# An attention and mixture-of-experts block: choosing the four experts by replacing them, finding slots by sorting, and keeping every routing weight behind its token's row

## What is computed

```python
scores = sigmoid(X @ gate_w.T)                       # 8192 x 32
_, idx = top_k(scores + bias, K)                     # four experts of a token
w = take_along_axis(scores, idx)                     # their scores, without the bias
w = w / clip(sum(w, -1), 1e-12)
eid = idx.reshape(-1)
pos = cumsum(onehot(eid)) - 1 at eid                 # how many came to this expert before
valid = pos < C                                      # later ones are dropped
xe[eid, pos] = X of the token, where valid
h  = silu(xe @ W1) * (xe @ W3);  ye = h @ W2         # each expert on its 512 slots
out = sum over the four choices of ye[eid, pos] * w  (0 where not valid)
out = out + silu(X @ sw1.T) * (X @ sw3.T) @ sw2.T    # shared expert
```

## Time and profile before

| | |
|---|---|
| median of three runs | 2133.41 us (2128.07, 2134.71, 2133.41) |
| the profiled execution | 2129.57 us |
| its span, first to last instruction | 2127.8 us |
| mean granted TensorE clock | 0.947 |
| busy share of the span: PE, DVE, ACT, POOL | 86%, 57%, 53%, 36% |
| first and last scatter of the routing (L1260) | start at 995.94 and 1451.96 us |
| first gather of the experts (L1412) | starts at 1456.45 us |

### The profile page before, as it was taken

How to read it: one execution, slowest core, us unless ns; L and a number is a source line. 1 busy time by engine, 2 the same in 40 slices (tenths; PEclk the granted TensorE clock), 3 DMA queues, 4 the chain that set the end, 5 groups by cost and what they waited for, 6 DMA issues and landing times.

```text
span 2127.8 us, 33721 instructions
## 1 busy us (share of the span) xinstructions
PE 1833.3 (86%) x12976; PEld 890.8 (42%) x12976; DVE 1207.1 (57%) x2230; ACT 1125.4 (53%) x1371; POOL 759.8 (36%) x718
## 2 busy tenths in 40 slices
PE   8899999999988999699788988545999989897785
PEld 6444444444436888123233333222444444443332
DVE  6676666666650000158788888861444434345886
ACT  5555554545525666568677777422444444442343
POOL 0000000000000000013787788875677777761110
PEclk9999999999998999899999999857999999999997
DMA  7435353455328887567787775443799999877983
GB/s 253 153 109 205 105 172 142 135 179 174 127 88 218 211 212 201 125 171 210 206 243 237 217 218 189 160 184 101 180 201 213 245 241 240 198 155 230 339 291 140
DMA packets 188848, 405.15 MB, mean 190 GB/s; under 512 B 33812, under 2 KB 72084, under 8 KB 172064
## 3 DMA queue, kind: packets, MB, share of 16 engines
q1 hardware_dynamic: 83184, 222.41, 35.4%
q10 hardware_dynamic: 68640, 124.26, 16.8%
q0 software_dynamic: 36864, 56.32, 13.9%
HBM read 237.06 MB, written 177.08 MB: 195 GB/s over the span
## 4 chain that ended last, share of the span: by engine, by line
PE 13%; DVE 12%; DMA 11%; issue 11%; POOL 8%; ACT 4%; SPq 1%; POOLq 0%; DVEq 0%; ACTq 0%
POOL slot_dram L1260 4%; PE s_gates L1485 3%; DMA acc_dram<-s_y,s_slot 3%; PE s_ups L1485 3%; DMA s_spread<-share_dram 2%; PE s_ys L1500 2%; DMA s_rows<-rows_dram,s_slot 2%; POOL acc_dram L1426 2%; DMA den_dram<-s_den 2%; ACT s_xT L1531 1%; DVE s_stats L1651 1%; DVE s_x L1670 1%; PE s_y L898 1%; PE s_turned L1462 1%; POOL s_rows L1412 1%
## 5 line engine op out<-in xcount | busy, mean ns | idle before, releaser
L258 PE MATMUL s_proj<-s_xT,keep_wqkv 128*128 128x512 f16 x1536 | 341.8, 379 | 0.0
L1260 POOL DMA_INDIRECT slot_dram<-keep_filled,keep_slots x256 | 293.4, 1146 | 98.2 <-issue 70.3
L1426 POOL DMA_INDIRECT acc_dram<-s_y,s_slot x128 | 202.9, 1585 | 96.2 <-DVE s_y L1627 42.1
L258 PEld LDWEIGHTS s_proj<-s_xT,keep_wqkv 128*128 128x128 f16 x1536 | 147.8, 98 | 183.2 <-issue 12.6
L898 PE MATMUL s_y<-keep_wo,s_at_hl 128*128 128x512 f16 x768 | 189.1, 399 | 37.7 <-ACT s_z L988 37.7
L237 PE MATMUL s_proj<-keep_wqkv,s_xT 128*128 128x512 f16 x768 | 180.5, 394 | 34.5 <-ACT s_xT L500 34.5
L1540 ACT ACTIVATE s_gate<-s_gates 128x512 f32<-128x512 f32 x96 | 57.1, 597 | 261.9 <-PE s_ups L1485 216.5
L339 POOL TENSOR_SCALAR s_rstd<-s_mv 128x4 f32<-128x4 f32 x16 | 16.0, 999 | 496.7 <-DVE s_mv L354 496.7
L1610 DVE SCALAR_TENSOR_TENSOR s_h<-s_gate,s_ups 128x512 f32<-128x512 f32 x96 | 65.8, 686 | 213.6 <-ACT s_gate L1540 213.6
L518 ACT ACTIVATE s_hl<-s_rot 128x1024 f16<-128x1024 f32 x64 | 67.6, 1057 | 221.8 <-DVE s_rot L400 221.3
L387 DVE TENSOR_TENSOR s_by_cos<-s_proj,s_table 128x1024 f32<-128x1024 f32 x64 | 78.3, 1224 | 172.2 <-PE s_proj L258 172.2
(11 more groups left out here) (165 smaller groups left out, 3209.8 us busy)
## 6 DMA issues: line engine op xcount, KB each, us to landing
s_x<-x_in SPq DMA_DIRECT2D x32, 1024.0 KB, 13.1
qk_dram<-s_hl ACTq DMA_DIRECT2D x32, 1024.0 KB, 5.9
keep_ahead<-qk_dram SPq DMA_DIRECT2D x48, 512.0 KB
acc_dram<-s_zero SPq DMA_DIRECT2D x17, 1024.0 KB, 11.2
v_dram<-s_v ACTq DMA_DIRECT2D x16, 1056.0 KB, 5.8
s_v<-v_dram SPq DMA_DIRECT2D x16, 1056.0 KB, 10.8
s_spread<-share_dram SPq DMA_DIRECT2D x64, 256.0 KB
x_dram<-s_x ACTq DMA_DIRECT2D x16, 1024.0 KB
```

The lines of the kernel that those rows point to most:

```text
L258: mm = nc.tensor.matmul(out[:, 512 * b:512 * b + 512], left, right, start=(c == 0 and i == 0), stop=(c == EC - 1 and i == 2))
L1260: nc.gpsimd.indirect_dma_start(out=io["slot"], out_offset=bass.IndirectOffsetOnAxis(ap=slots[n % 2][:, a * K + j:a * K + j + 1], axis=0), ...
L1426: nc.gpsimd.indirect_dma_start(out=io["acc"], out_offset=bass.IndirectOffsetOnAxis(ap=slot[e % RING][:, a, 0:1], axis=0), in_=y[e % 2][:, ...
```

## The change

The routing keeps one column per expert where it had one per choice. choose still sorts with MAX8, then replaces the four best scores by a number that no score has (match_replace with `NEVER`, the other four entries of its list being `-NEVER`), and the mask is where that number stands: index, chosen, onehot and picked are gone. weigh multiplies score and mask (128 x 4 x 32), sums, and divides. The slots come by sorting: read_position now makes `away` (a large number less the expert's base and less the position) and `taken` (position under 512 and chosen); fill multiplies them, and MAX8 brings the four nonzero ones of 32 to the front. The order of a token's choices is thereby that of its slots, so a scatter can no longer carry a choice's weight. It writes the token number alone (4 bytes); all 32 weights of each token are stored by ACT behind the token's row (store_weights, a new DMA per group), rows are gathered with them (2176 bytes instead of 2048), and DVE copies an expert's column out (take_weight) before it scales that expert's results. FILL and SEND are one step earlier.

```diff
-        SCORE, CHOOSE, PLACE, WEIGH, FILL, SEND = 18, 18, 19, 19, 21, 21
+        SCORE, CHOOSE, PLACE, WEIGH, FILL, SEND = 18, 18, 19, 19, 20, 20
...
             def store_rows(n):
                 act.wait_ge(x_low_ready, A * (n + 1))
-                act.dma_start(io["rows"][n * G:(n + 1) * G, :].rearrange("(a p) n -> p a n", p=P),
-                              hl[n % 2][:].rearrange("p a s e -> p a (s e)")).then_inc(rows_stored[n % 2], 16)
+                act.dma_start(io["rows"][n * G:(n + 1) * G, 0:E].rearrange("(a p) n -> p a n", p=P),
+                              hl[n % 2][:].rearrange("p a s e -> p a (s e)").bitcast(U32)).then_inc(rows_stored[n % 2], 16)
+
+            def store_weights(n):
+                act.wait_ge(weights_ready, n + 1)
+                act.dma_start(io["rows"][n * G:(n + 1) * G, E:ROW].rearrange("(a p) n -> p a n", p=P),
+                              weights[n % 2][:].bitcast(U32)).then_inc(weights_stored[n % 2], 16)
...
+                n = group_at(s, WEIGH + 1)
+                if n is not None:
+                    store_weights(n)
...
                 for a in range(A):
-                    ins = nc.vector.max(top[:, a, :], biased[:, a, :])
+                    ins = nc.vector.max(top[:, a, 0:8], biased[:, a, :])
                 then(ins)
                 for a in range(A):
-                    ins = nc.vector.max_index(index[:, a, :], top[:, a, :], biased[:, a, :])
+                    best = top[:, a, :].rearrange("p (b j) -> p b j", j=K)[:, 0:3:2, :]
+                    ins = nc.vector.match_replace(left_over[:, a, :], best, biased[:, a, :], NEVER)
                 then(ins)
-                then(nc.vector.tensor_copy(chosen[:], index[:, :, 0:K]))
-                then(nc.vector.tensor_tensor(onehot[:], number, chosen[:].unsqueeze(3).broadcast_to([P, A, K, NE]),
-                                             ALU.is_equal))
-                with nc.allow_low_precision(reason="sums of zeros and one 1"):
-                    ins = nc.vector.tensor_reduce(mask[:], onehot[:].rearrange("p a j e -> p a e j"), AX.X, ALU.add)
-                ins.then_inc(mask_ready, 1)
+                nc.vector.tensor_scalar(mask[:], left_over[:], NEVER, None, ALU.is_equal).then_inc(mask_ready, 1)
 
             def weigh(n):
-                then(nc.vector.tensor_tensor(picked[:], onehot[:], per_choice(score[:]), ALU.mult))
-                then(nc.vector.tensor_reduce(w[:], picked[:], AX.X, ALU.add))
-                then(nc.vector.tensor_reduce(weight_sum[:], w[:], AX.X, ALU.add))
+                k = n % 2
+                dve.wait_ge(mask_ready, n + 2)
+                if n >= 2:
+                    dve.wait_ge(weights_stored[k], 16 * (n // 2))
+                then(nc.vector.tensor_tensor(weights[k][:], score[:], mask[:], ALU.mult))
+                then(nc.vector.tensor_reduce(weight_sum[:], weights[k][:], AX.X, ALU.add))
...
             def read_position(n):
+                at = position.rearrange("p (a e) -> p a e", e=NE)
                 dve.wait_ge(position_ready, n + 1)
-                nc.vector.tensor_copy(where[:].rearrange("p a e -> p (a e)"), position).then_inc(where_ready, 1)
+                nc.vector.tensor_tensor(away[:], first, at, ALU.subtract).then_inc(where_ready, 1)
+                nc.vector.scalar_tensor_tensor(out=taken[:], in0=at, scalar=float(CAP), in1=mask[:], op0=ALU.is_lt,
+                                               op1=ALU.mult).then_inc(where_ready, 1)
...
-                then(nc.vector.tensor_scalar(far[:], where[:], float(CAP), NOWHERE, ALU.is_ge, ALU.mult))
-                then(nc.vector.tensor_tensor(slot[:], where[:], first, ALU.add))
-                then(nc.vector.tensor_tensor(slot[:], slot[:], far[:], ALU.add))
-                then(nc.vector.tensor_tensor(picked[:], onehot[:], per_choice(slot[:]), ALU.mult))
-                then(nc.vector.tensor_reduce(place[:], picked[:], AX.X, ALU.add))
+                dve.wait_ge(where_ready, 2 * n + 2)
+                then(nc.vector.tensor_tensor(away[:], away[:], taken[:], ALU.mult))
+                nc.vector.tensor_reduce(ours[:], mask[:].rearrange("p a e -> p e a"), AX.X, ALU.add)
+                for a in range(A):
+                    ins = nc.vector.max(last[:, a, :], away[:, a, :])
+                then(ins)
...
-                        in_=filled[n % 2][:].bitcast(U32)[:, a, j, :], in_offset=None, bounds_check=NSLOT - 1,
+                        in_=keep["token"][:, m:m + 1], in_offset=None, bounds_check=NSLOT - 1,
...
-        slot = [t.sb(f"slot{r}", [P, A, 2], U32) for r in range(RING)]
-        rows = [t.sb(f"rows{r}", [P, A, 2 * E], F16) for r in range(AHEAD)]
+        slot = [t.sb(f"slot{r}", [P, A], U32) for r in range(RING)]
+        rows = [t.sb(f"rows{r}", [P, A, ROW], U32) for r in range(AHEAD)]
...
+            def take_weight(e):
+                r = e % AHEAD
+                dve.wait_ge(gathered[r], 16 * A * (e // AHEAD + 1))
+                if e >= AHEAD:
+                    dve.wait_ge(y_copied, A * (NS + e - AHEAD + 1))
+                nc.vector.tensor_copy(weight[r][:], rows[r][:].bitcast(F32)[:, :, E + e]).then_inc(weight_ready, 1)
...
                     low(NS + e + 1, i)
+                if e + 2 < NE:
+                    take_weight(e + 2)
                 down(e)
```

More of the change, by code:

```diff
@@ L25 @@
 KR = 3 * D + 2
-NOWHERE = 1.0e6
+NOWHERE = float(1 << 20)
+NEVER = 3.0e38
+ROW = E + NE
 ALU = mybir.AluOpType
@@ L794, in attend_and_route_programs @@
         gates, position = route[:, 0:A * NE], route[:, A * NE:2 * A * NE]
-        q_loaded, xT_stored, rows_stored, scattered = (
-            [t.sem(f"{n}{k}") for k in range(2)] for n in ("q_loaded", "xT_stored", "rows_stored", "scattered"))
+        q_loaded, xT_stored, rows_stored, weights_stored, scattered = (
+            [t.sem(f"{n}{k}") for k in range(2)]
+            for n in ("q_loaded", "xT_stored", "rows_stored", "weights_stored", "scattered"))
         x_loaded, x_stored = ([t.sem(f"{n}{r}") for r in range(XS)] for n in ("x_loaded", "x_stored"))
@@ L808, in attend_and_route_programs @@
                                "gates_ready"))
-        score_ready, mask_ready, position_ready, where_ready, step, slots_ready = (
-            t.sem(n) for n in ("score_ready", "mask_ready", "position_ready", "where_ready", "step", "slots_ready"))
+        score_ready, never_set, mask_ready, position_ready, where_ready, step, weights_ready, slots_ready = (
+            t.sem(n) for n in ("score_ready", "never_set", "mask_ready", "position_ready", "where_ready", "step", "weights_ready",
+                               "slots_ready"))
         UNITS = NT + ADD - MEASURE
@@ L920, in make_gates @@
                     if a == 2:
[L921 removed]
+                        pe.wait_ge(where_ready, 2 * n)
                 for c in range(EC):
@@ L1070, in dve_program @@
         def dve_program(dve):
-            number = keep["expert"][:, 0:NE].unsqueeze(1).unsqueeze(1).broadcast_to([P, A, K, NE])
-            first = keep["expert"][:, NE:2 * NE].unsqueeze(1).broadcast_to([P, A, NE])
+            first = keep["expert"][:].unsqueeze(1).broadcast_to([P, A, NE])
             bias = keep["bias"][:].unsqueeze(1).broadcast_to([P, A, NE])
@@ L1193, in fill @@
-                nc.vector.tensor_copy(filled[k][:].bitcast(U32)[:, :, :, 0],
-                                      keep["token"][:, n * A:(n + 1) * A].unsqueeze(2).broadcast_to([P, A, K]))
-                nc.vector.tensor_copy(slots[k][:], place[:].rearrange("p a j -> p (a j)")).then_inc(slots_ready, 1)
+                nc.vector.tensor_scalar(slots[k][:].rearrange("p (a j) -> p a j", j=K), last[:, :, 0:K], -1.0, NOWHERE,
+                                        ALU.mult, ALU.add).then_inc(slots_ready, 1)
@@ L1197, in dve_program @@
+                then(nc.vector.tensor_tensor(before_us[:], before_us[:], ours[:], ALU.add))
             for k in range(2):
@@ L1312, in expert_and_combine_programs @@
         x1 = [t.sb(f"x1{r}", [P, A, E]) for r in range(X1S)]
-        total = [y[0][:], y[1][:]] + [r[:].rearrange("p a n -> p (a n)").bitcast(F32).rearrange(
-            "p (a e) -> p a e", a=A) for r in rows]
+        total = [y[0][:], y[1][:]] + [r[:].bitcast(F32)[:, :, 0:E] for r in rows]
         stats, mv = t.sb("stats", [P, A, 6]), t.sb("mv", [P, A, 2])
@@ L1674, in dve_program @@
                 for a in range(A):
-                    nc.vector.memset(rows[r][:, a, :], 0.0).then_inc(cleared, 1)
+                    nc.vector.memset(rows[r][:].bitcast(F32)[:, a, :], 0.0).then_inc(cleared, 1)
             for i in range(IC):
@@ L1684, in dve_program @@
                 copy_early(p)
+            take_weight(0)
             for i in range(IC):
@@ L1687, in dve_program @@
                 low(NS, i)
+            take_weight(1)
             for e in range(NE):
@@ L1771 @@
     "xT2": ([NG, P, 2 * EC * G], F16),
-    "rows": ([T, 2 * E], F16),
-    "slot": ([NSLOT, 2], U32),
+    "rows": ([T, ROW], U32),
```

(6 more changed lines are left out.)

45 lines of the change are left out of this document (21 added, 24 removed).

## The result

The changed kernel takes 2202.28 us (median of four runs, 2190.73 to 2210.69) beside 2132.31 us for the kernel before: a ratio of 1.0325, 95% interval 1.0294 to 1.0355. It is 70 us slower, where 2122 us, 2106 to 2137, had been predicted. The profiled execution took 2201.68 us, its span is 2199.9 us.

A forecast was written before the change was run, and what follows sets the result against it. DVE's own work and the denominators' DMA trip were taken to bound attention turns, PE the experts. Turns -9.6, tail -5.1, experts +4 make -10.7 us on 2129.57 profiled; plus 3.84 for the median, 2122 us (2106 to 2137).

The forecast's parts named there:

- the tail: POOL's scatters after the last rstd: 40 instead of 44 by sending one step earlier, -5.1 us; 4-byte scatters priced as 8-byte.
- the twelve turns: Attention-stage loop, division to division: weigh's .9 us gain less .1 for the weights' store, -.8 a turn, -9.6 us.
- The first rival: Attention loop: weights' store and closer stores lengthen denominator round trips by .8 us a turn, 2132 us; chance .22 with late fill.
- an uncovered trip of 8.74 us: Early attention turn with less traffic: make_share to division took 8.74 us, DVE waiting 2.81 for spread; full turns over 11.
- The first part of the turn: Division to end of read_total, set by DVE's work alone: falls from 10.0 to 9.1 us through a shorter weigh.
- The experts: Expert stage: gathered rows of 2176 bytes for 2048 lengthen PE's waits for rows, +4 us, ends 0 and 8.5.
- The dearer gather: Rival, expert stage: odd-length gathers take 1588 ns instead of 1053, POOL sets the pace, +37 us, 2140 to 2156; chance .12.
- POOL closing the loop: Rival, attention loop: denominator trips fall until POOL limits turns at 28.7 us; 2113 us (2114.9 or 2111); chance .12.

## Why the prediction was wrong

**The step that failed** stands in the tail's paragraph: "The 4-byte scatter is priced as the 8-byte one; POOL's time is for its 128 rows." POOL's time is indeed the same (1146 ns a scatter on average before, 1147 after). But a scatter was priced by its issuing engine, and by its packets, and neither shows what its writes do to others: that term stood at nothing without a reason. In its place the twelve turns, forecast at -9.6 us, came to +75, 70 of them in SP's waits for the stores of den and share. That sorting changes which places one scatter writes was not considered at all. The tail's other term, -5.1 us for sending a step earlier, came out as +22 with 4-byte elements. Against the base with 32 bytes the runs give the price of places closer than that (us):

| | old order | sorted |
|---|---|---|
| old kernel, 8 bytes | 2131 - 2117 = 14 | 2153.5 - 2117 = 36 |
| old kernel, 4 bytes | 2151 - 2117 = 34 | not run |
| changed kernel, 8 bytes | not run | 2171 - 2106 = 65 |
| changed kernel, 4 bytes | not run | 2202 - 2106 = 96 |
| changed kernel, 4 bytes, sent a step later | not run | 2180 - 2112 = 68 |

(2131 and 2117 are the medians of before and of its 32-byte run, measured together; 2106 is the changed kernel's with 32 bytes, 2112 the same sent a step later.) In the old kernel the order and the closer places add some 20 us each to its 14: 56. Sent at the same step, the changed kernel pays 68, not far from that, its two runs being 15 us apart; the other 28 come with the early sending. Why that makes the close places dearer was not tested.

**The first rival** had the mechanism, longer trips that give the gain back, but took the weights' store, and stores closer together, for the cause and .8 us a turn for the price; it was 6.2 us a turn (75 us in twelve), and the weights' store costs nothing that shows. The early turn with an uncovered trip of 8.74 us had shown that traffic alone moves it.

**The first part of the turn: right.** The match_replace rows, and a weigh with the read_total behind it, changed kernel, DVE in order of time:

```profile
1177.72 0.09 DVE L1166 MATCH_VALUE_LOAD s_left_over<-s_top,s_biased 128x8 f32 x1
1177.80 0.18 DVE L1166 MATCH_REPLACE8 s_left_over<-s_top,s_biased 128x32 f32<-128x32 f32 x1
...
1178.49 0.23 DVE L1168 TENSOR_SCALAR s_mask<-s_left_over 128x128 f16<-128x128 f32 x1
1181.62 2.29 DVE L1108 TENSOR_TENSOR s_heads<-s_heads,s_spread 128x2048 f32<-128x2048 f32 x1 [2.90 <-DMA s_spread<-share_dram]
...
1186.52 0.27 DVE L1175 TENSOR_TENSOR s_weights<-s_score,s_mask 128x128 f32<-128x128 f32 x1
...
1187.77 2.29 DVE L1112 TENSOR_TENSOR s_at_hl<-s_heads,s_at_hl 128x2048 f16<-128x2048 f32 x1
1189.97 0.68 DVE L1096 TENSOR_SCALAR s_den<-s_total 128x512 f32<-128x512 f32 x1
```

Match_replace takes what FIND_INDEX8 took (.18), weigh 1.25 us for a predicted 1.38, and from the division to the end of read_total it is 9.03 us for a predicted 9.1, 10.03 before.

**The tail: about half.** POOL in order of time, changed kernel: the last rstd, a scatter of the last group, the last scatter, the first gather.

```profile
1467.99 0.72 POOL L1261 TENSOR_TENSOR s_rstd<-s_rstd,s_power 128x2 f32<-128x2 f32 x1
...
1483.72 0.97 POOL L1268 DMA_INDIRECT slot_dram<-keep_token,keep_slots  x1 [2.80 <-issue]
...
1522.82 0.97 POOL L1268 DMA_INDIRECT slot_dram<-keep_token,keep_slots  x1 [0.30 <-issue]
1527.38 1.05 POOL L1422 DMA_INDIRECT s_rows<-rows_dram,s_slot  x1 [3.59 <-DMA s_slot<-slot_dram]
```

54.8 us from the last rstd to the last scatter instead of 57.6: 40 scatters as predicted, but 2.8 us of waiting before 1483.72, just after the last group's slots were made at 1482.01. In time, with the list spaced, sending a step later costs 5.8 us by the medians above.

**The experts: nothing instead of +4.** From the first gather to the end the nine profiles with rows of 2176 bytes lie between 667.3 and 678.7 us, the five with rows of 2048 between 668.2 and 674.8. The estimate from the Trainium skill's page (DMA: Bandwidth & Descriptors, How a descriptor splits into AXI transactions), up to 13 us more, does not show in any run. The dearer gather did not come: 1038 ns on average in 400 us of the stage, 1053 before. PE's waits for rows did not grow either: 11.1 us there, 17.1 before.

**POOL closing the loop: right for the spaced list.** That rival had said 28.7 us a turn and 2111 to 2115 us. With 32 bytes the last ten turns average 28.8 us, and the time is 2106; from 1040 to 1320 us POOL waits for another engine 5.1 us in all, 15.7 before. So the gain of the change was there, 11 us beside an equally spaced kernel before; it lay under 96 us of held-up writes. That the prediction's sum had -10.7 is luck in part: by the two profiled executions with 32 bytes the twelve turns give -6.6 us (forecast -9.6), the way from the last division to the first gather -3.8 (tail -5.1), and the experts -2.5, within their spread (+4).

**Readings of the prediction that were off, without deciding it.** The 13 ns "of just such pieces" is the time of a packet of q0, and 5093 packets for ten turns are 32 for a scatter of 128 elements. Half of the experts' queue was taken for gathers; its bytes grew from 50.31 to 51.54 MB, which at 6.25% makes them 39%. An expert was given 13.14 us; from gather to gather it is 13.9, which leaves the dearer gather's +37 us nearly as it is.

Busy time, length and engines as in the earlier trace rows, from 1000 to 1200 us; kernel before:

```profile
1000.00:1200.00 200.00, 169.71 (x1321) 63.11 (x1320) 167.97 (x425) 149.86 (x190) 153.92 (x155) 0.97 0.80 228
```

Changed kernel:

```profile
1000.00:1200.00 200.00, 135.48 (x975) 49.09 (x974) 105.56 (x299) 110.62 (x141) 103.86 (x112) 0.82 0.85 170
```

Changed kernel with 32 bytes:

```profile
1000.00:1200.00 200.00, 181.98 (x1436) 68.22 (x1432) 152.76 (x433) 162.84 (x209) 160.92 (x166) 0.99 0.79 246
```

All engines fall together in the changed kernel while the DMA engines are busier (.85) and move less (170 GB/s): here that goes with transfers that wait, not with more work. The mean granted TensorE clock of that stretch, in which PE is idle for a third of the time, is .82, so part of it ran at the lower level, 1.2 GHz; with the list spaced it is .99.

## What to carry to other kernels

Price a scatter by where its writes land, not by its issue or its packets: if neighbours are written close together in time, try small scattered elements 32 bytes apart, even though it moves more bytes. When a reordering (a sort, a different tie-break) feeds an indirect DMA, ask which addresses one DMA now writes, and count them on the real indices: an even drawing was assumed here, and two thirds of the choices are in fact dropped. If DMA engines get busier and move less while an untouched queue's packets grow longer, look among the small writes of the other queues.

## What the runs showed of the hardware

Elements written by indirect DMA to close places held up another queue's stores: SP's waits for two of them went from 73.2 to 143.5 us, one of 32 KB from 1.5 to 11.7. In the changed kernel the cost falls by 30 to 35 us per doubling of the distance between 4 and 32 bytes, and depends little on the element's own size (2114.68 us for 4 bytes 32 apart, 2106.32 for 32 bytes). Sorting the destinations alone, in the same list, cost 21 us. In contrast 512 pieces of 128 bytes a turn, 2176 bytes apart, cost nothing that could be measured (ratio .9995, .9969 to 1.0021). Whether more than 32 bytes would give more, whether the length of the list has a part in it, and which part of the path to HBM holds the writes, stays open.
